# A sandwich block of latent attention and feed-forward on one core: first query tiles scored unsplit, six value-output products computed in the first stage, and two steps of the start reordered

## The reference, cut to what matters

```
q   = rmsnorm(x @ Wq_a, w) @ Wq_b          # rank 192, 32 heads, 128 plain + 64 rotated features
ckv = x @ Wkv_a                            # 64 compressed, 64 rotated features
kv  = rmsnorm(ckv[:64], w) @ Wkv_b         # per head 128 for keys, 128 for values
scores = (qf @ kf.T) * scale;  causal mask;  softmax
o   = probs @ v;   attention = o @ Wo
x   = x + layernorm(attention)
x   = x + layernorm(ffn(layernorm(x)))     # two gated projections with low-rank parts, one down
```

## Time and profile before

| | us |
|---|---|
| median of 3 runs | 595.21 (594.8 to 596.28) |
| profiled execution, its own time | 596.79 |
| span in the profile | 594.8 |
| granted TensorE clock, mean | 0.991 of full |
| TensorE busy | 562.7 (95%) |
| VectorE busy | 447.6 (75%) |
| ScalarE busy | 399.8 (67%) |
| GpSimd busy | 214.2 (36%) |

### The profile page before, as it was taken

The page is one execution under the profiler, slowest core; times in us unless marked ns, Lnnn a source line. Parts: engine busy times, 40 slices in busy tenths (PEclk is TensorE's granted clock), DMA queues, the critical chain, the costliest instruction groups (busy, mean ns, idle before and its releaser), DMA issues. The chain is left out here.

```text
span 594.8 us, 10807 instructions
## 1 busy us (share of the span) xinstructions
PE 562.7 (95%) x3336; PEld 432.8 (73%) x3336; DVE 447.6 (75%) x1203; ACT 399.8 (67%) x1157; POOL 214.2 (36%) x204
## 2 busy tenths in 40 slices
PE   4789999999999999999999999999889999979996
PEld 4677778777787787787787877876568888745564
DVE  4886787787777777777877877778668889878466
ACT  4456778787887787787878877877653455355444
POOL 2234354444444543544444445432000000036520
PEclk9998999999999999999999999999999999999998
DMA  8101223213312322222123123025490000101003
GB/s 333 35 1 32 76 70 106 77 51 94 108 49 77 108 68 77 71 103 77 51 94 108 49 81 108 33 78 175 168 357 10 1 1 1 31 1 53 1 18 125
DMA packets 19560, 46.92 MB, mean 79 GB/s; under 512 B 2608, under 2 KB 3120, under 8 KB 19248
## 3 DMA queue, kind: packets, MB, share of 16 engines
q1 hardware_dynamic: 19504, 46.23, 23.4%
HBM read 39.80 MB, written 6.42 MB: 78 GB/s over the span
## 5 line engine op out<-in xcount | busy, mean ns | idle before, releaser
L694 DVE CUSTOM_DVE_ANT_0 ss<-bank,cst 128x128 f32<-128x128 f32 (+3 forms) x256 | 125.2, 490 | 85.0 <-PE bank L1036 64.1
L435 ACT ACTIVATE pt<-bank 128x128 f32<-128x128 f32 (+3 forms) x256 | 109.9, 429 | 65.5 <-PE bank L1078 65.2
L427 ACT ACTIVATE pr<-ss,small 128x128 f32<-128x128 f32 (+3 forms) x256 | 142.5, 557 | 6.3 <-DVE small L694 3.7
L329 POOL TENSOR_TENSOR qrot<-qrot,qswp 64x512 f32<-64x512 f32 x64 | 82.2, 1284 | 104.2 <-DVE qrot L686 101.7
L1078 PE MATMUL bank<-ident,pr 128*128 128x128 f32 x640 | 114.3, 276 | 1.0 <-ACT pr L427 0.9
L336 POOL TENSOR_TENSOR qt_lo<-qrot,qt_hi 128x512 fp32r<-128x512 f32 x64 | 82.1, 1283 | 69.8 <-ACT qt_hi L417 68.6
L1034 PE MATMUL bank<-kt_hi,qt_hi 128*128 128x128 f32 (+3 forms) x256 | 100.3, 392 | 1.8 <-DVE small L694 1.3
L1078 PEld LDWEIGHTS bank<-ident,pr 128*128 128x128 f32 x640 | 77.0, 141 | 22.4 <-issue 5.3
L1036 PE MATMUL bank<-kt_hi,qt_lo 128*128 128x128 f32 (+3 forms) x256 | 83.0, 324 | 0.0
L1035 PE MATMUL bank<-kt_lo,qt_hi 128*128 128x128 f32 (+3 forms) x256 | 82.7, 323 | 0.0
L1090 PE MATMUL bank<-pt,kvn 128*64 128x256 f32 (+3 forms) x512 | 75.2, 436 | 0.7 <-ACT pt L435 0.7
(11 more groups left out here) (163 smaller groups left out, 1068.7 us busy)
## 6 DMA issues: line engine op xcount, KB each, us to landing
sv<-sv SPq DMA_DIRECT2D x16, 576.0 KB, 4.4
rsb<-rinv_scratch SPq DMA_DIRECT2D x64, 128.0 KB, 2.9
sq<-sq SPq DMA_DIRECT2D x16, 448.0 KB, 3.4
wvo_scratch<-vs SPq DMA_DIRECT2D x16, 256.0 KB, 2.2
wv_raw<-wvo_scratch SPq DMA_DIRECT2D x8, 512.0 KB, 4.4
xa<-x SPq DMA_DIRECT2D x8, 256.0 KB, 5.4
x<-x SPq DMA_DIRECT2D x1, 2048.0 KB, 10.0
out<-yo SPq DMA_DIRECT2D x8, 256.0 KB, 2.0
```

What stands on the lines that cost most here:

```text
L329: nc.gpsimd.tensor_tensor(qrot[RKV:P, h, :], qrot[RKV:P, h, :], qswp[RKV:P, h, :], ALU.add)\
L427: nc.scalar.activation(pr[:, k % 4, 0:n], ss[:, RING[k], 0:n], ACT.Exp, bias=negmax[:, k % 8:k % 8 + 1], scale=-1.0, accum_out=rsum[:, k:k ...
L435: nc.scalar.activation(pt[:, b, h, 0:i + 1, i * P:(i + 1) * P], bank[2 + k % 2][:, 0:(i + 1) * P].rearrange("p (j q) -> p j q", q=P), ACT. ...
L694: nc.vector.tensor_tensor_reduce(out=ss[:, RING[k], 0:n], in0=bank[k % 2][:, 0:n], in1=mask[:, SEQ - n:SEQ], scale=-SCALE, scalar=3.4e38, ...
```

## The change

1. `scores` for i = 0 is one product of the unsplit query tile `qrot[:, h, 0:128]` with an unsplit key tile `kt1` (L1101 after), in place of three products of split tiles. It waits for `pe_added`; the wait for `qt_split` moves to i = 1. ScalarE copies `kt1` twice in the first stage (128x128, blocks 0 and 4). `query_hi` and `query_lo` split 384 columns in place of 512.
2. The value-output products of pairs 0 to 5 are made in the first stage: at the end of TensorE's iterations t = 4, 5, 6, two at t = 7, and one at t = 10, into banks that are free there. Six loads `sve` stand ahead of the load of `sv` for pair 6. ScalarE's copies (`move_early`) stand between the square root L532 and the copy `xt_hi` of the iterations 5, 6, 7, two at 8, and one behind t = 11; they go to `pr`, `ss` and `vs` and from there to DRAM. TensorE's first queries wait for the fifth copy, ScalarE's first exponentials for the stores. In the attention, pair p makes the product of pair p + 6, and pairs 10 to 15 make none.
3. ScalarE runs a one-column Exp at t = 10 ahead of its first wait for a mask. VectorE rotates the second query behind the second mask (t = 11) in place of t = 9, and ScalarE splits it behind the second exponential.
4. `kra`, `krb`, `sqj` lie elsewhere in SBUF.

```diff
@@ -46,6 +46,8 @@
...
 PU = BATCH * UNITS
+EARLY = {4: ((0, 7, 0),), 5: ((1, 7, 1),), 6: ((2, 7, 2),), 7: ((3, 7, 3), (4, 6, 0)), 10: ((5, 2, 0),)}
+NE = 6
 HID, RANK = 1376, 2
...
@@ -118,6 +120,8 @@
...
     r8 = qswp[0:2 * QB, 0, 0:P]
+    sve = Map(nc, att.at - 4 * 4 * QB * SEQ, att.at).take("sve", [P, NE, SV_COLS])
+    early = [pr[:, j, :] for j in range(4)] + [ss[:, 2, :], vs[:, :]]
     negmax = small[:, 0:8]
...
@@ -129,14 +133,15 @@
...
     fi2 = Map(nc, att.at, top)
+    kt1 = fi2.take("kt1", [P, BATCH, P])
     wa = fi2.take("wa", [P, DC, LAT])
...
     kcs = fi2.take("kcs", [P, QB, 2, ROPE])
-    kra = fi2.take("kra", [P, TB, ROPE])
-    krb = fi2.take("krb", [P, TB, ROPE])
-    sqj = fi2.take("sqj", [P, 2, RQ])
+    kra = fir.take("kra", [P, TB, ROPE])
+    krb = fir.take("krb", [P, TB, ROPE])
+    sqj = fir.take("sqj", [P, 2, RQ])
     st1 = fi2.take("st1", [P, TB, 16])
...
@@ -205,8 +210,10 @@
...
         x_turned xt_hi_made xt_split wa_hi_made wa_split lat_made squares_summed std_rms_made rstd_rms_made
-        q_scaled q_doubled qn_made krot_parts kvn_made qk_turned qk_hi_made qk_split""")
+        q_scaled q_doubled qn_made krot_parts kvn_made kt1_made qk_turned qk_hi_made qk_split""")
     rope = lambda k: sq[:, SQ_COLS - 4 * ROPE:SQ_COLS].rearrange("p (k h n) -> p k h n", k=2, h=2)[:, k]
+    sve_in = [nc.alloc_semaphore(f"sve_in{j}") for j in range(NE)]
+    early_out = [nc.alloc_semaphore(f"early_out{j}") for j in range(NE)]
     x_in = [nc.alloc_semaphore(f"x_in{t}") for t in range(TB)]
...
@@ -235,7 +242,9 @@
...
             sp.dma_start(cst[:, :], cst_d).then_inc(f.cst_in, 16)
-            sp.dma_start(sv[:, :], sv_d[0]).then_inc(a.sv_in, 16)
+            for j in range(NE):
+                sp.dma_start(sve[:, j, :], sv_d[j]).then_inc(sve_in[j], 16)
+            sp.dma_start(sv[:, :], sv_d[NE]).then_inc(a.sv_in, 16)
             def send_r(m):
...
@@ -262,34 +271,34 @@
...
 
-            load_sq(1)
-            load_sq(2)
-            send_r(0)
-            load_sv(1)
-            store_wvo(0)
-            for p in range(1, PAIRS - 2):
-                send_r(2 * p - 1)
-                load_sq(p + 2)
+            for j in range(NE):
+                if j == 2:
+                    load_sq(1)
+                sp.wait_ge(a.wvo_moved, j + 1)
+                sp.dma_start(wvo_d[j], early[j]).then_inc(early_out[j], 16)
+            for p in range(PAIRS - 1):
+                if p:
+                    send_r(2 * p - 1)
+                if p + 2 < PAIRS:
+                    load_sq(p + 2)
                 send_r(2 * p)
-                load_sv(p + 1)
-                store_wvo(p)
-            send_r(2 * PAIRS - 5)
-            send_r(2 * PAIRS - 4)
-            load_sv(PAIRS - 1)
-            store_wvo(PAIRS - 2)
+                if p + NE + 1 < PAIRS:
+                    load_sv(p + NE + 1)
+                if p + NE < PAIRS:
+                    store_wvo(p + NE)
             send_r(2 * PAIRS - 3)
...
                     send_r(2 * PAIRS - 2)
-                if k == 4:
-                    store_wvo(PAIRS - 1)
                 if k >= 3:
...
                     send_r(2 * PAIRS - 1)
-                    sp.wait_ge(a.wvo_out, 16 * PAIRS)
+                    sp.wait_ge(a.wvo_out, 16 * (PAIRS - NE))
+                    for out in early_out:
+                        sp.wait_ge(out, 16)
                 sp.dma_start(wv_raw[:, k % 3, :, :], wvo_d[2 * k:2 * k + 2].rearrange("a p n -> p a n"))\
...
@@ -333,7 +342,7 @@
...
                 pool.wait_ge(a.qt_hi_made, gi + 1)
-                nc.gpsimd.tensor_tensor(qt_lo[:, b, h, :], qrot[:, h, :], qt_hi[:, b, h, :].bitcast(F32), ALU.subtract)\
+                nc.gpsimd.tensor_tensor(qt_lo[:, b, h, P:SEQ], qrot[:, h, P:SEQ], qt_hi[:, b, h, P:SEQ].bitcast(F32), ALU.subtract)\
                   .then_inc(a.qt_split, 1)
...
@@ -414,7 +423,7 @@
...
                     act.wait_ge(a.s_made, s_done)
-                nc.scalar.activation(qt_hi[:, b, h, :], qrot[:, h, :], ACT.Copy).then_inc(a.qt_hi_made, 1)
+                nc.scalar.activation(qt_hi[:, b, h, P:SEQ], qrot[:, h, P:SEQ], ACT.Copy).then_inc(a.qt_hi_made, 1)
 
...
@@ -507,9 +516,11 @@
...
                         query_hi(4 * p + 4 + h, 0, h, PU * p + QB * (h + 1))
-                    if k == 10:
-                        act.wait_ge(a.wvo_made, p + 1)
-                        if not first:
+                    if k == 10 and p + NE < PAIRS:
+                        act.wait_ge(a.wvo_made, p + NE + 1)
+                        if first:
+                            act.wait_ge(early_out[NE - 1], 16)
+                        else:
                             act.wait_ge(a.wvo_out, 16 * p)
...
@@ -518,6 +529,12 @@
...
                 nc.scalar.activation(st1[:, t, 8:9], st1[:, t, 7:8], ACT.Sqrt, bias=eps_ln).then_inc(f.std_made, 1)
+
+            def move_early(t):
+
+                for j, b, _ in EARLY[t]:
+                    act.wait_ge(a.wvo_made, j + 1)
+                    nc.scalar.activation(early[j], bank[b][:, :], ACT.Copy).then_inc(a.wvo_moved, 1)
 
...
@@ -531,6 +548,8 @@
...
                       .then_inc(f.std_rms_made, 1)
+                if 4 <= t - 1 < TB:
+                    move_early(t - 1)
                 if 0 <= t - 1 < TB:
...
@@ -542,6 +561,8 @@
...
                     act.wait_ge(f.qk_turned, u + 1)
+                    if u % QB == 0:
+                        nc.scalar.activation(kt1[:, u // QB, :], tq[:, 2 * P:3 * P], ACT.Copy).then_inc(f.kt1_made, 1)
                     nc.scalar.activation(ql_hi[:, :, u * P:(u + 1) * P],
...
@@ -554,13 +575,18 @@
...
                     weights_hi(0, first=True)
-                if t in (TB + 1, TB + 3):
-                    h = (t - TB - 1) // 2
-                    query_hi(h, 0, h)
+                if t == TB + 1:
+                    query_hi(0, 0, 0)
                 if t == TB + 2:
+                    nc.scalar.activation(eps[:, 3:4], eps_ln, ACT.Exp)
+                    act.wait_ge(early_out[0], 16)
                     exponent(0, 0, True)
 
+            move_early(TB + 2)
+            for j in range(1, 4):
+                act.wait_ge(early_out[j], 16)
             exponent(1, 1, True)
+            query_hi(1, 0, 1)
             body(0, first=True)
...
@@ -683,6 +709,7 @@
...
                     dve.wait_ge(a.qt_split, gi - 1)
+                    dve.wait_ge(a.s_made, QB * (gi - 2) + 1)
                 nc.vector.tensor_tensor(qrot[:, h, :], bank[6 + h][:, :], cos1, ALU.mult).then_inc(a.q_rotated, 1)
...
@@ -829,12 +856,14 @@
...
                     dve.wait_ge(f.cst_in, 16)
-                if t in (TB, TB + 1):
-                    rotate_swapped(t - TB, t - TB, first=True)
-                    rotate_own(t - TB, t - TB, first=True)
                 if t in (TB + 2, TB + 3):
                     mask_and_max(t - TB - 2, t - TB - 2, first=True)
-
+                if t in (TB, TB + 3):
+                    h = (t - TB) // 3
+                    rotate_swapped(h, h, first=True)
+                    rotate_own(h, h, first=True)
+
+            dve.wait_ge(early_out[4], 16)
             body(0, first=True)
...
@@ -1061,9 +1090,17 @@
...
                 if i == 0:
+                    pe.wait_ge(a.pe_added, gi + 1)
+                    if U in (0, UNITS):
+                        pe.wait_ge(f.kt1_made, b + 1)
+                if i == 1:
                     pe.wait_ge(a.qt_split, gi + 1)
...
                     pe.wait_ge(a.s_masked, U - 1)
+                if i == 0:
+                    nc.tensor.matmul(bank[k % 2][:, 0:P], qrot[:, h, 0:P], kt1[:, b, :], start=True, stop=True)\
+                      .then_inc(a.s_made, 1)
+                    return
                 keys = slice(b * SEQ, b * SEQ + (i + 1) * P)
...
@@ -1098,13 +1135,24 @@
...
 
-            def absorb_output(p):
-
-                pe.wait_ge(a.sv_in, 16 * (p + 1))
+            def absorb_output(j, b=XB, w=sv):
+
+                pe.wait_ge(a.sv_in if j >= NE else sve_in[j], 16 * (j - NE + 1) if j >= NE else 16)
                 for h in range(2):
-                    last = nc.tensor.matmul(bank[XB][RKV * h:RKV * (h + 1), :], sv[:, h * RKV:(h + 1) * RKV],
-                                            sv[:, 2 * RKV + h * D:2 * RKV + (h + 1) * D], start=True, stop=True)
+                    last = nc.tensor.matmul(bank[b][RKV * h:RKV * (h + 1), :], w[:, h * RKV:(h + 1) * RKV],
+                                            w[:, 2 * RKV + h * D:2 * RKV + (h + 1) * D], start=True, stop=True)
                 last.then_inc(a.wvo_made, 1)
+
+            def absorb_early(t):
+
+                for j, b, moved in EARLY[t]:
+                    if moved:
+                        pe.wait_ge(a.wvo_moved, moved)
+                    if b == 6:
+                        pe.wait_ge(a.wq_split, 1)
+                    if b == 2:
+                        pe.wait_ge(f.qn_made, TB - 1)
+                    absorb_output(j, b, sve[:, j, :])
 
...
@@ -1131,23 +1179,23 @@
```

(16 more changed lines are left out.)

## The result

| | before | after |
|---|---|---|
| median, first comparison (4 runs each) | 595.75 us | 588.80 us |
| ratio, 95% interval | | 0.9864 (0.9829 to 0.9900) |
| profiled execution, own time | 596.79 | 590.17 |
| span | 594.8 | 588.2 |

The kernel is 7.0 us faster, 1.4%. 585.1 us was forecast, 580 to 590 the range. The time lies in the range, and 3.7 us above the forecast, so it is outside the band of 582 to 588 that the prediction gave its likeliest outcome.

What follows compares the result with a forecast made beforehand. TensorE was taken to bound the attention, fully busy at full clock. Tiles -5.0, value-output products -5.5, splits and queue 0, start +0.4 gave -10.1: from 595.2 to 585.1 us, range 580.0 to 590.0.

Steps and rivals of the forecast that it cites:

- The tiles: First query tiles in the attention: one unsplit product takes 0.21 us in place of 0.29, 5.0 us over 63 tiles.
- rival A: Three paced products become two, 6.9 us less, and the start gains 1.5: 581.3 us; chance 0.22.
- D: Rival: the unsplit product runs as four paced passes, 0.44 us in 63 tiles, slower than before: 599.6 us; chance 0.05.
- The value-output products: Attention pairs 10 to 15 make none, saving TensorE 6 x 0.91 = 5.5 us.
- The splits: ScalarE and GpSimd split 384 columns in place of 512; both wait for others in the attention: 0.
- the earlier release: Tile i = 0 is released earlier, by `pe_added`; TensorE never waits there in the attention: 0.
- the queue of SP: Six early loads ahead of pair 6's `sv` land before use, and the delayed `sq` load is in time: 0.
- The start: First stage: early products delay queries, the moved rotation compensates; +0.4 us in all, between -1.5 and +4.2.
- B: Rival: the start pays for the early products, +4.2 us in place of +0.4: 588.9 us; chance 0.13.
- the table load: ScalarE's load before the first exponential, 42.10 to 43.38 before: hidden ahead of the mask wait as before, or just not.
- The tail: Behind the attention's last `output`: shifts whole with what precedes it; first 13.5 us, to 436.25's counterpart, stay.
- The sum: Whole kernel: -5.0 - 5.5 + 0 + 0.4 = -10.1 us, put on the median 595.2, giving 585.1 us.

Runs made afterwards that it cites:

- experiment 8: The changed kernel with the second query's rotation back at t = 9, ahead of the last block's scaling: 590.48 us, ratio 0.9889.
- experiment 9: The changed kernel with five early value-output products in place of six, only one at t = 7: 589.25 us, ratio 0.9867.
- experiment 10: The changed kernel without the one-column Exp ahead of the first mask: 590.54 us, ratio 0.9881.
- experiment 4: The changed kernel with three split products for tile i = 0 again, early products and reordered start kept: 592.98 us, ratio 0.9923.
- experiment 6: The changed kernel with ScalarE's copy `wd_hi` moved from G = 8 to G = 10, behind `xf_hi`: 587.74 us, ratio 0.9835.
- experiment 12: The changed kernel with 128 more waits (64 instructions) at the head of TensorE's program: 588.73 us, ratio 0.9848.
- experiment 3: The kernel before with only the unsplit i = 0 tile and what belongs to it: 593.78 us, ratio 0.9943.
- experiment 1: The changed kernel measured again without an edit: 589.89 us, ratio 0.9871.

## Why the prediction was right, and what was off

**The tiles.** Right. 0.08 us a tile was forecast, 0.071 measured; 63 of them are 4.5 us in place of 5.0. The sum over five matmuls was the better basis than their single starts (10.1 us) or a price of 0.11 us for each of three (rival A's 6.9, and the 6.7 from weight loads): three split products take 0.29 us, the unsplit one 0.22. D's time of 0.44 us is refuted; what happens inside the two records of 0.11 us no run shows.

**The value-output products.** Right: 0.88 us each in place of 0.91.

**The splits, the earlier release, the queue of SP.** Forecast 0, and nothing in the three numbers needs them: 352.58 us or within 0.02 of it stands between the marks in six profiles of five programs, whose starts differ by up to 1.4 us.

**The start.** The schedule was met closely: `kt_hi` ends at 36.5 (36.3 forecast), the last block's scaling is at 43.0 (43.1), the third mask at 48.8 (49.2), the first `move_p` at 50.8 (51.0), the fourth exponential at 51.8 (near 52), and TensorE keeps its clock at 44 to 48 us. Against the first profile of before the first mark is 0.7 us earlier, where the sum had +0.4. But the size of this term depends on the execution that one compares with: the first marks of before are 60.7 and 59.6 with the lost clock, 58.5 and 58.3 without it, those of after 60.0 and 59.9. So the start costs about 1.5 us against an undisturbed execution (50.05 us from the first latent product to the first mark, in place of 48.55 and 48.61) and gains 0.7 against the one the prediction was worked out on; that it came out as a gain there is luck. B's mechanism is real, at a third of its price; that the time, 588.8, is nearly B's 588.9 is a coincidence, since most of what is missing is missing in the tail. The pieces, by experiments 8, 9 and 10: the moved rotation -0.3, the second product of t = 7 +1.1, and the Exp ahead of the mask -1.1 against a loss that the change itself would have made. TensorE kept full clock in the start in all eight profiles that have both the early products and the unsplit tile, and in two of the four with the old program.

The forecast of the table load, "hidden as before, or just not", was right for the kernel as it is, but I had not seen what the Exp is there for.

**The tail.** Here the prediction failed. Its step was: "That tail is counted from the last `output`, so what comes before it shifts it whole." It does not: 175.4 and 175.6 us after, 171.4 to 172.6 before. Two mechanisms, told apart by experiments 4, 6 and 12, and the clock behind them:
- The packet of TensorE's instructions moved into the load of `wd`: it lands 1.1 to 1.6 us later in the two profiles of after, and 0.8 to 1.3 us of TensorE's idle time go with it (2.40 and 2.87 us, against 1.57 in experiment 12). Shown: 64 instructions that compute nothing take it out again.
- `xf_lo` of VectorE and `fs` of GpSimd meet. Before, VectorE's takes 0.67 and GpSimd's is stretched to 1.93; in all changed kernels it is 1.26 to 1.32 for GpSimd and 1.64 to 1.77 for VectorE. TensorE waits for VectorE's: about 1.0 us. The sums fit one waiting for the other: 1.26 + 0.67 = 1.93. The Trainium skill, page "SBUF — State Buffer", section "SBUF: two separate sides", calls the pair of ports that the two engines share an exclusive lock, held for a whole instruction by whichever starts first. The durations agree, the recorded starts do not tell who wins: they are 0.09 to 0.17 us apart in favour of GpSimd in both kinds of kernel, and in the old ones it is GpSimd's instruction that is stretched. Why the order turned is open.

Together they idle TensorE for 2.4 to 3.5 us, in place of 0.52. The third part is the clock, and it is the largest. From the matmul behind that wait to the end of the span it is 50.15 to 50.20 us in the six profiles in which the clock did not fall there, and 51.68 to 51.79 in the eight in which it did: 1.5 us. The length of the wait does not decide it. Behind 2.61 us it fell (experiment 3) and behind 2.64 it did not (experiment 8, tail 174.3); behind 1.59 it fell (experiment 4) and behind 1.57 it did not (experiment 12). So of the 2.2 us between the tails of experiments 1 and 12, 1.6 are the clock, and that the moved packet saved it is not shown.

**The sum.** On the two first profiles: -9.45 - 0.73 + 3.6 = -6.6, the difference of the spans. With the tail unchanged it would have been -10.2 against -10.1 forecast. Against the forecast the medians miss 3.1 us (first comparison) and 2.6 (experiment 1).

**Open.** The four profiled executions of old programs took 593.9 to 596.8 us, while the medians of before in the later comparisons are 597.1 to 597.4. Part of it is the clock, of which each timed execution has its mean on record: the twelve timed executions of before with 0.989 or less took 597.6 to 600.0 us, the six with 0.997 or more 593.9 to 597.1. Where in those executions it fell is in no profile, and what else differs is open. Against the mean of profiled executions the change gains less (5.2 us) than against the medians (7.5).

## What to carry to other kernels

A change that removes instructions from a long unrolled program also moves the packets that fetch the rest of it; where one of them falls on a short load that an in-order engine waits for, a stage that was not touched gets slower. So count the tail behind a change as unchanged only if its waits for DMAs have slack, and move such a wait behind the work that others need: here one line took 0.8 to 1.2 us from TensorE's idle time, and the median fell by 2.1 us, which is hardly clear of noise. And before an activation of another function, look at how many waits it has: here, with two, the table load landed behind the first. And before a difference between two profiles is put down to an edit, look whether both started alike: here the late landing of one block of x looked like 1.1 us of gain.
